# Two causal attentions and a mixture of experts on one core: unrolled attention steps, four narrow tiles for the softmax sums, and two additions given to GpSimd

## The reference, cut to what matters

```python
x = x + layernorm(attn(layernorm(x)))     # attention 1: 16 heads of 64, causal
x = x + layernorm(ffn(layernorm(x)))

def ffn(x):
    h = rmsnorm(x, ln1_w)
    q, k, v = split(h @ wqkv.T)           # attention 2: 16 query heads, 4 key heads of 16
    q, k = apply_rope(q), apply_rope(k)   # t * cos + rot(t) * sin
    x = x + softmax(causal(q @ k.T * 0.25)) @ v @ wo.T
    h = rmsnorm(x, ln2_w)
    w, e = top2(softmax(h @ gate_w.T))    # 8 experts, 2 for each token
    return x + sum(w[j] * w2[e[j]] @ (silu(w1[e[j]] @ h) * (w3[e[j]] @ h)) for j in (0, 1))
```

## Time and profile before

| | |
|---|---|
| time, median of 3 runs | 2839.74 us (2831.24 to 2841.79) |
| the profiled execution's own time | 2830.77 us, its span 2829.0 us |
| TensorE busy | 2436.7 us, 86% |
| VectorE busy | 1638.5 us, 58% |
| ScalarE busy | 1463.6 us, 52% |
| GpSimd busy | 909.7 us, 32% |

### The profile page before, as it was taken

The page is one execution under the profiler, slowest core; times in us unless marked ns, Lnnn a source line. Parts: engine busy times, 40 slices in busy tenths (PEclk is TensorE's granted clock), DMA queues, the critical chain, the costliest instruction groups (busy, mean ns, idle before and its releaser), DMA issues. The chain is left out here.

```text
span 2829.0 us, 56112 instructions
## 1 busy us (share of the span) xinstructions
PE 2436.7 (86%) x12338; PEld 1395.4 (49%) x12339; DVE 1638.5 (58%) x4355; ACT 1463.6 (52%) x3189; POOL 909.7 (32%) x1663
## 2 busy tenths in 40 slices
PE   4999999999999999999836599999988839999980
PEld 2555566555655556555523233333333726666650
DVE  5666654666546664666368677777775462222227
ACT  3566553656445663656338477777776522222222
POOL 0344432444334443444404122222222023333320
PEclk8999999999999999999968699999999859999995
DMA  2010010001000110010124211111111521111114
GB/s 100 17 28 27 23 43 15 18 27 42 24 19 23 27 33 24 19 28 27 26 67 172 94 27 30 30 33 33 33 33 28 189 106 45 44 46 44 45 48 167
DMA packets 132932, 134.67 MB, mean 48 GB/s; under 512 B 65792, under 2 KB 102400, under 8 KB 131072
## 3 DMA queue, kind: packets, MB, share of 16 engines
q1 hardware_dynamic: 123712, 109.57, 12.6%
q0 software_dynamic: 6912, 18.88, 2.0%
q10 hardware_dynamic: 2112, 4.19, 0.4%
HBM read 87.50 MB, written 33.82 MB: 43 GB/s over the span
## 5 line engine op out<-in xcount | busy, mean ns | idle before, releaser
L1222 ACT ACTIVATE b_P<-b_SC 128x512 f32<-128x512 f32 (+3 forms) x768 | 333.3, 496 | 173.6 <-PE b_SC L1325 171.5
L296 POOL TENSOR_TENSOR a_A<-a_A,a_P 128x512 f32<-128x512 f32 (+3 forms) x320 | 322.6, 1008 | 305.0 <-PE a_O L600 291.8
L448 ACT ACTIVATE a_P<-a_SC 128x512 f32<-128x512 f32 (+3 forms) x640 | 293.2, 469 | 225.8 <-PE a_SC L583 185.1
L506 DVE CUSTOM_DVE_ANT_0 a_MX<-a_MX,a_causal 128x128 f32<-128x128 f32 (+3 forms) x512 | 249.8, 500 | 201.5 <-PE a_MX L649 190.2
L582 PE MATMUL a_SC<-a_QR,a_KR 128*128 128x512 f32 (+3 forms) x768 | 319.2, 419 | 7.2 <-DMA a_QS<-a_minusT 2.9
L649 PE MATMUL a_MX<-a_KR,a_QR 128*128 128x512 f32 (+3 forms) x768 | 289.9, 386 | 14.5 <-DVE a_peak L506 10.7
L1374 PE MATMUL b_MX<-b_K,b_Q 96*128 96x512 bf16 (+3 forms) x768 | 252.2, 340 | 50.1 <-ACT b_Q L1233 16.4
L1164 POOL TENSOR_SCALAR_AFFINE_SELECT b_P<-b_P 128x128 f32<-128x128 f32 x512 | 147.2, 293 | 458.6 <-ACT b_P L1222 451.0
L1272 DVE CUSTOM_DVE_ANT_0 b_MX<-b_MX,b_causal 128x128 f32<-128x128 f32 (+3 forms) x512 | 249.9, 498 | 69.2 <-PE b_MX L1374 62.6
L583 PE MATMUL a_SC<-a_QS,a_KS 65*128 65x512 f32 (+3 forms) x768 | 265.2, 349 | 0.0
L1948 PE MATMUL e_GU<-W,e_hT 128*128 x576 | 261.9, 598 | 1.0 <-ACT e_hT L2000 0.8
(11 more groups left out here) (258 smaller groups left out, 4075.2 us busy)
## 6 DMA issues: line engine op xcount, KB each, us to landing
a_inv<-inv_rows SPq DMA_DIRECT2D x128, 128.0 KB, 2.9
stack_rows<-p_stk SPq DMA_DIRECT2D x32, 480.0 KB, 2.6
a_W<-in_w_pair SPq DMA_DIRECT2D x34, 384.0 KB, 3.5
b_stk<-stack_rows SPq DMA_DIRECT2D x136, 96.0 KB, 1.9
W<-in_w SPq DMA_DIRECT2D x8, 1024.0 KB, 5.8
n_x<-in_x SPq DMA_DIRECT2D x4, 1024.0 KB, 9.4
a_xT<-hold SPq DMA_DIRECT2D x4, 1024.0 KB, 4.7
p_x<-in_x SPq DMA_DIRECT2D x4, 1024.0 KB, 9.5
```

What stands on the lines that cost most here:

```text
L296: eng.tensor_tensor(acc[h][c][:, a:], acc[h][c][:, a:], buffer(n, h)[:, a:], ALU.add).then_inc(added[h], 1)
L448: act.activation(buffer(n, h)[:, a:], SC[h][:, a:], ACT.Exp, scale=DH1 ** -0.5).then_inc(s["exp_done"], 1)
L506: dve.tensor_tensor_reduce(MX[c % MAX_BANKS1][:, 0:w], MX[c % MAX_BANKS1][:, 0:w], causal[:, BANK - w:], 1.0, 3 * NEG, ALU.add, ALU.max, p ...
L1222: act.activation(probs[k % RING2][:, a:], SC[k % SCORE_BANKS][:, a:], ACT.Exp, scale=DH2 ** -0.5).then_inc(s["exp_done"], 1)
```

## The change

- In both attentions the loops are gone: all steps are written out, so that every wait and address is a constant.
- In attention_one the sums of one chunk are four matmuls of 32 columns over 256 queries each, instead of two of 64 columns over 512. ScalarE copies 256 columns instead of 512, and SyncE folds four half rows instead of two rows.
- `NORM_SLOT` of chunk 1 goes from 7 to 9, `WO_SLOT` from 6 to 7.
- In project_two the sum of the two rotary products goes from VectorE to GpSimd; GpSimd's loop goes by rounds, with both sums of a round ahead of the third parts of the round before.
- In combine the last addition goes from VectorE to GpSimd.

```diff
-NORM_SLOT = (2, 7)
-WO_SLOT, WO_GROUPS = 6, ST_N // 2
+NORM_SLOT = (2, 9)
+WO_SLOT, WO_GROUPS = 7, ST_N // 2
 FOLD = BANK // P
+HALF = BANK // 2
+SUM_ROWS = 32
...
-            with eng.Fori(0, B - 1) as b:
-                n = b * PAIRS
-                steps(n, PAIRS // 2 - 1)
-                step(n + (PAIRS + 1), n + PAIRS, n + (PAIRS - 1), n + (PAIRS - 2), 0, begins=True)
-                step(n + (PAIRS + 2), n + (PAIRS + 1), n + PAIRS, n + (PAIRS - 1), 1, wo=b)
-            steps(N - PAIRS, PAIRS // 2 - 2)
-            step(N - 1, N - 2, N - 3, N - 4, 0)
+            for m in range(N - 3):
+                r = (m + 2) % PAIRS
+                step(m + 3, m + 2, m + 1, m, m % 2, begins=r == 0, wo=m // PAIRS if r == 1 else None)
...
-                for h in range(2):
-                    sp.dma_start(fold[c][:, h, :], total[c][DH1 * h:DH1 * h + 1, :]).then_inc(folded[c], 16)
+                for part in range(2):
+                    for h in range(2):
+                        row = SUM_ROWS * (2 * part + h)
+                        sp.dma_start(fold[c][P // 2 * part:P // 2 * (part + 1), h, :], total[c][row:row + 1, :]).then_inc(folded[c], 16)
...
-                            act.activation(total[c][:, :], sum_bank[c][:, :], ACT.Copy).then_inc(s["sums_copied"], 1)
+                            act.activation(total[c][:, :], sum_bank[c][:, 0:HALF], ACT.Copy).then_inc(s["sums_copied"], 1)
...
-                for h in range(2):
-                    last = pe.matmul(sum_bank[c][DH1 * h:DH1 * (h + 1), :], ones[:, :], acc[h][c][:, :], start=True, stop=True)
+                for part in range(2):
+                    for h in range(2):
+                        row = SUM_ROWS * (2 * part + h)
+                        last = pe.matmul(sum_bank[c][row:row + SUM_ROWS, 0:HALF], ones[:, :], acc[h][c][:, HALF * part:HALF * (part + 1)],
+                                         start=True, stop=True)
...
+            def rotate(t, i):
+                pool.wait_ge(s["crossed"], t * 3 + 3)
+                pool.tensor_tensor(rot[i][:, :], rot[i][:, :], crs[i][:, :], ALU.add).then_inc(s["rotated"], 1)
...
-                for u in range(2):
-                    dve.wait_ge(s["crossed"], (r * 2 + u) * 3 + 3)
-                    dve.tensor_tensor(rot[2 * p + u][:, :], rot[2 * p + u][:, :], crs[2 * p + u][:, :], ALU.add).then_inc(s["rotated"], 1)
-
...
-            with eng.Fori(0, STEPS2 // 2 - 1) as u:
-                step(u * 2 + 2, u * 2 + 1, u * 2, 0)
-                step(u * 2 + 3, u * 2 + 2, u * 2 + 1, 1)
+            for n in range(2, STEPS2):
+                step(n, n - 1, n - 2, n % 2)
...
-                for t in range(Q4 * i, Q4 * (i + 1)):
-                    dve.wait_ge(s["y_ready"], t + 1)
-                    dve.tensor_tensor(rows[:, t, :], Y[t % 4][:, :], rows[:, t, :], ALU.add).then_inc(s["row_ready"], 1)
+
+        @block.gpsimd
+        def _(pool):
+            for t in range(NT):
+                pool.wait_ge(s["y_ready"], t + 1)
+                pool.tensor_tensor(rows[:, t, :], Y[t % 4][:, :], rows[:, t, :], ALU.add).then_inc(s["row_ready"], 1)
```

More of the change, by code:

```diff
@@ L216, in attention_one @@
         acc = [[sb(f"a_A{h}{c}", [P, BANK]) for c in range(2)] for h in range(2)]
-        total = [sb(f"a_total{c}", [P, BANK]) for c in range(2)]
+        total = [sb(f"a_total{c}", [P, HALF]) for c in range(2)]
         inv = [sb(f"a_inv{c}", [P, BANK]) for c in range(2)]
@@ L224, in attention_one @@
         ident = sb("a_ident", [P, P])
-        ones = sb("a_ones", [P, DH1])
+        ones = sb("a_ones", [P, SUM_ROWS])
         causal = sb("a_causal", [P, BANK])
@@ L256, in run @@
         def run(eng, step, end=lambda: None):
-            def steps(first, count):
-                with eng.Fori(0, count) as u:
-                    m = first + u * 2
-                    step(m + 3, m + 2, m + 1, m, 0)
-                    step(m + 4, m + 3, m + 2, m + 1, 1)
             step(0, None, None, None, 1)
@@ L837, in _, with third, step @@
             pool.memset(V2, 1.0).then_inc(s["ones_set"], 1)
-            with pool.Fori(0, NT // 4) as g:
-                for i in range(4):
-                    pool.wait_ge(s["second_set"], (g * 4 + i) * 2 + 2)
-                    r = rot[i][:, :].rearrange("p (h d) -> p h d", d=DH2)
-                    for lo, hi, parts in ((0, H2, Q_PARTS), (H2, HEADS2, K_PARTS)):
-                        pool.tensor_tensor(stk[i][:, lo:hi, parts.index(2), :], r[:, lo:hi, :],
-                                           stk[i][:, lo:hi, parts.index(1), :], ALU.subtract).then_inc(s["third_set"], 1)
+            def rotate(t, i):
+                pool.wait_ge(s["crossed"], t * 3 + 3)
+                pool.tensor_tensor(rot[i][:, :], rot[i][:, :], crs[i][:, :], ALU.add).then_inc(s["rotated"], 1)
+            def third(t, i):
+                pool.wait_ge(s["second_set"], t * 2 + 2)
+                r = rot[i][:, :].rearrange("p (h d) -> p h d", d=DH2)
+                for lo, hi, parts in ((0, H2, Q_PARTS), (H2, HEADS2, K_PARTS)):
+                    pool.tensor_tensor(stk[i][:, lo:hi, parts.index(2), :], r[:, lo:hi, :],
+                                       stk[i][:, lo:hi, parts.index(1), :], ALU.subtract).then_inc(s["third_set"], 1)
+            def step(r, p):
+                for u in range(2):
+                    rotate(r * 2 + u, 2 * p + u)
+                if not (isinstance(r, int) and r == 0):
+                    for u in range(2):
+                        third((r - 1) * 2 + u, 2 * (1 - p) + u)
+            pairs(pool, step)
+            for u in range(2):
+                third(NT - 2 + u, 2 + u)
         def tile_of(t, n, k):
@@ L915, in cross @@
                 dve.wait_ge(s["third_set"], t * 2 + 2)
+                dve.wait_ge(s["rotated"], t + 1)
                 C = cos[:, bass.ds(t % ST_N, 1), :].to_broadcast([P, HEADS2, DH2])
```

4 lines of the change are left out of this document (2 added, 2 removed).

## The result

The changed kernel takes 2746.11 us (median of 4 runs, 2744.12 to 2752.26), the kernel before on the same chip 2838.6 us. The ratio is 0.9676, with a 95% interval from 0.9656 to 0.9696. The forecast was 2748 us. The profiled execution took 2745.91 us, its span is 2744.2 us against 2829.0, and so 84.8 us are gone.

What follows compares the result with a forecast made beforehand. TensorE was taken to bound attention_one, a ring of waits project_two, TensorE and VectorE attention_two, VectorE's chain combine. -50 -21 +1 -8 -12 +2 = -88 us on 2830.8 gives 2743, plus half of 9 us: 2748 us; range 2712 to 2795.

Steps and rivals of the forecast that it cites:

- The loops of attention_one: Attention_one: writing out the loops removes nested-step register work, jumps back and the stall at the inner loop's end; -50 us.
- (a): Attention_one: 19 plain steps in the nested loops each lose 1.2 us to register work; 23 us.
- (b): Attention_one, steps with the Wo projection: two jumps back at 7.2 us, 14 us, and register work in six intervals, 7 us.
- (c): Attention_one: leaving the inner loop for the last steps stalls, 42.7 us against 37.1; 5.5 us.
- The sums: Attention_one: narrower groups of sums hold TensorE 0.57 us instead of 0.97, 64 times; 26 us, taken as -21.
- The moved slots: Attention_one: the wait for V's copy goes, -5.3 us; a new 2 us wait of TensorE comes three times, +6; net +1.
- Project_two: Project_two: rotary sums on GpSimd release ScalarE and VectorE sooner, 0.55 us in each of 15 rounds; -8 us.
- Combine: Combine: GpSimd's additions hold up VectorE's mixing by what it is spared; the last quarter's additions are slower; +2 us.
- Only the jumps and the sums: Rival, chance 0.22: register work is hidden behind the engines' work, the last sequence is faster for another reason; 2782 us.
- Everything tighter: Rival, chance 0.13: without register work, 32 plain steps of attention_one go 0.9 us lower each; 2719 us.
- The other engines become the bound: Rival, chance 0.11: the sums' gain becomes waits for exponentials and masks, project_two gains nothing, combine +6; 2781 to 2789 us.
- Fetching cannot keep up: Rival, chance 0.04: written-out steps of attention_one each stall once on new code, 29 x 7.2 = 209 us; 2957 us.

## Why the prediction was right, term by term

The sum was -88 us on the profiled execution, the trace shows -84.8. The terms are not all as good as the sum.

- *The loops of attention_one, forecast -50.* Put back alone they cost 38.4 us. (a) is right: 1.24 us a nested step against the 1.2 I took, 20 us in the steps between the projections (21.5 without the first one, in which the changed kernel's trace had the lower clock and the nested one's not); and the cause is as said, since with one loop register the steps are at 36.5. (b) was mis-sized in both its parts: -21 forecast, +10.6 when put back. The register part was taken at 7 us for three pairs; the pair without a jump shows some 0.5 us of it, and the other 1.7 of its 2.3 us are the lower clock. The jumps were taken at 7.2 us each, which is what a pair across a jump is over one without in the kernel before; when the loops are put back it is 2.6 and 2.9 us. The stall on TensorE's queue is not smaller: from the branch to the next instruction 3.6 us at both jumps before, and 3.8 and 4.6 us put back. But in the kernel before TensorE ran out of issued matmuls 0.4 us behind the branch and stood for 4.15 us, and the four matmuls behind that took 3.78 us, while the granted clock, which had fallen in the pause, was at the lower level. By stretch, before:

```profile
457.00:464.00 7.00, 4.90 (x8) 2.64 (x9) 1.37 (x2) 0.04 (x1) 0.99 (x1) 0.51 0.18 44
```

  With the loops put back it has 3.5 us of issued matmuls left at the branch. At the first jump it stands for 1.27 us, the clock stays at 1.00 and the same four take 1.98 us; at the second it stands for 2.07 us, with a clock of 0.60 for the next 4 us:

```profile
450.36 1.98 PE L630 MATMUL a_PV<-hold,a_W 128*128 x4 [1.27 <-issue]
```

  A jump's price is not its own: here it went with how much work stood issued ahead of it and with the clock behind the pause. Why more stands issued here wasn't tried apart. (c) had the right size (6.5 us for 5.5) and the wrong name: not leaving the loop but one jump back stalls.
- *The sums, -21.* Put back alone they cost 24.0 us. The shading from 26 was in the right direction and a little too strong; that the four folds cost nothing holds within this.
- *The moved slots, +1.* The parts alone, 38.4 and 24.0, make 62.4, and the trace has 62.7: what is left for the slots is about nothing. This nothing is a balance, and no run has the old slots in written-out code to show them alone. The three waits of 2 us are there to the tenth, and the fourth at the stage's end and the clock behind the pauses I had missed. Against them stand the three waits of 1.77 us for the copy of V, which are gone, and some 9 us by which the two jumps had already become cheaper in the kernel with loops and moved slots. By this working (an estimate: 38.4 and 9) the loops were worth some 47 us in the kernel before, and the slots cost some 9; which of the two terms was off depends on the order in which they are taken.
- *Project_two, -8.* -6.4 in the trace, which is the fastest of the nine with this form; -5.3 by their mean. Rounds are 5.5 us on average, not the 5.1 that I had named as a sign, and ScalarE still waits 0.53 us. The step that was too kind is that only ScalarE's and VectorE's relief counted; GpSimd's third parts now meet VectorE's rest (0.69 us for an instruction of 0.21).
- *Attention_two, -12.* -15.9. The jumps are as forecast, some 1.2 us each, but there are six and not seven: 7 us for 8. The register work was taken at 0.25 us a step and is 0.66, some 9 us in the looped steps for 4.
- *Combine, +2.* 0. The mechanism is right (10.17 us for the forecast's 10.7; 0.7 us an addition in the last quarter). It came out 2 us better because the three quarters keep 0.6 us each of what VectorE was spared.

So a term too large by nearly 12 us, against one too small by 4, the sums 3 short and combine 2 better, gave a sum that is right within 3 us. This was in part luck; and the even balance of slots and jumps inside attention_one was not foreseen either.

The rivals. "Only the jumps and the sums" falls by the two runs with loops in attention_one: register work costs where two registers enter. "Everything tighter" had 0.9 us more a step for removing the last register; the steps show 36.4 to 36.6 us with one register and 36.34 with none, 0.1 to 0.2 us. (In attention_two, where the last register is worth 0.66 us, it would have been nearer.) "The other engines become the bound" did not come in attention_one: TensorE's waits for VectorE are 12.2 us in all. "Fetching cannot keep up" falls with the same view, which has no wait of TensorE by "issue".

The Trainium skill ("SBUF — State Buffer", section Who interferes with whom) was weighed against this change at combine: a VectorE instruction with two SBUF inputs and a GpSimd instruction that reads SBUF lock each other out. The traces agree, with 480 ns alone and up to 948 ns beside an addition, and with the additions back on VectorE combine takes 65.5 us against 65.4. On jumps the Trainium skill says ("Runtime: NRT & Kernel Launch", section Instruction fetch mechanics) that a taken branch whose target is no longer held stalls, while code in sequence is fetched ahead. The long loop agrees: all four engines stop for 3.9 to 4.2 us at the jump of the six-step body, and in the written-out steps of attention_one from 100 to 1290 us no engine waits more than 0.4 us by "issue" (weight loads, which run ahead of their matmuls, aside).

## What to carry to other kernels

Before writing a loop out, look at how many loop registers enter the waits and addresses of its body: writing out the outer loop alone gave all but a few microseconds of what writing out both gave in attention_one. What a jump costs can't be read off one place: look at the branch and the next instruction on every queue, at what stands issued ahead of it, and at the granted clock behind it. An addition moved to GpSimd is free only if VectorE does nothing with two SBUF inputs beside it; and when a slot is moved ahead of another engine's wait, count what now stands before it, at the stage's end as well.

## What the runs showed that I had not expected

- One loop register instead of two takes TensorE's register instruction from 138 to 55 ns, and a step of attention_one from 37.58 to 36.5 us. No register at all brings only 0.1 to 0.2 us more there, but 0.66 us a step in attention_two.
- The same jump of the same kind of body stalls VectorE's queue for 0.3 us in one place and 4.2 us in another of the same kernel.
- In attention_two a body of six steps costs 4.8 us at its one jump, one of two steps 1.2 us at each: fewer jumps of a longer body brought 4 us (599.5 against 603.7 us for the stage), and writing out 13 more.
- A wait of VectorE for its own earlier sums, some 0.1 us of pause ahead of each product, made project_two 4.5 us longer (112.9 against 108.4 us); rounds come in two lengths, 5.5 and 6.1 us, and it made nearly all the longer.
- A pause of 1.99 us of TensorE was followed by a granted clock of 0.90 in one place and of 1.00 in two others; the lower clock cost 1.7 us more. Much of the 9 us between traces of the same attention_one is of this kind.
